# Row-tile pipeline for the self-attention layer norms in a perceiver layer, with the centring moved into the weights

## The chip, the cores and the metric

One core of a Trainium2 chip runs the whole kernel as one launch. The metric is the device time of that launch in microseconds (us). The kernel before took 1715.89 us, the median of 3 runs that lay between 1709.82 and 1721.77. Lower is better.

## The reference

The kernel computes one perceiver layer on 512 latent rows of width 512 and a context of 8192 rows: cross attention with 16 heads of 32, then self attention, then a mixture of 8 experts. The change touches the second step and the weights it uses, so that part is what must be seen:

```python
def layernorm(x, w, b):                      # over the 32 columns of one head
    mu = jnp.mean(x, axis=-1, keepdims=True)
    var = jnp.mean((x - mu) ** 2, axis=-1, keepdims=True)
    return (x - mu) * jax.lax.rsqrt(var + LN_EPS) * w + b
Q = split_heads(jnp.einsum('bsd,od->bso', x, W_Q))
K = split_heads(jnp.einsum('bsd,od->bso', x, W_K))
V = split_heads(jnp.einsum('bsd,od->bso', x, W_V))
Q = layernorm(Q, q_ln_w, q_ln_b)
K = layernorm(K, k_ln_w, k_ln_b)
scores = jnp.einsum('bhqd,bhkd->bhqk', Q, K) / jnp.sqrt(jnp.float32(hd))
attn = jax.nn.softmax(scores, axis=-1)
context = jnp.einsum('bhqk,bhkd->bhqd', attn, V)
v_weights = sparse_W_V.mean(axis=2)          # one vector per head
z = jnp.einsum('bnd,hd->bhn', context_flat, v_weights)
z_sparse = top_k_activation(z, TOP_K)        # the 128 largest of each row
o_weights = sparse_W_O.mean(axis=1)
y_flat = jnp.einsum('bhn,hd->bnd', z_sparse, o_weights)
```

The mean of a head's 32 outputs is linear in the weights: subtracting from every column of the (transposed) weights the mean over its head's 32 columns gives centred outputs.

## The kernel before, in words

The program is a sequence of stages, each a block in which every engine has its own list of instructions, written out in order. A stage begins when every engine has ended the one before. Semaphores alone order the engines among themselves; there is no planner.

- **First pass** (`project_context`): keys and values of the context are projected and stored to DRAM, and the row maxima of the scores are found.
- **Second pass** (`attend_context`, about 572 to 1176 us): for each of 4 groups `g` of 4 heads, 64 tiles `T` of 128 context rows. For each tile TensorE makes the scores (L665), ScalarE takes the exponentials into one of 6 slots of `att_pr` (L748), TensorE multiplies them with the values (L679), and VectorE adds the tile to a running sum of exponentials (`att_tot`, L798, 128 by 2048 elements, both inputs in SBUF). A group has 7 runs of 9 or 10 tiles; the first tile of a run costs no addition, so a 9-tile run has 8 additions. After a run, four tiles later, TensorE sums `att_tot` over its partitions (L695), for which it waits until the additions of that run are done. ScalarE may write a slot only when the addition of the tile six before is done. At a group's end VectorE copies the output out of PSUM (L824) before TensorE may write that bank again. A few tiles into the next group VectorE inverts the sums (L805) and GpSimd multiplies them in (L593, L595). GpSimd also writes the two rows with the next group's maxima into `g_stacks` (L589), which TensorE needs before the next group's first scores.
- **End of the second pass**: after the last additions TensorE sums once more, then computes the output projection and the transposes of the normalised rows (`g_hT`).
- SyncE's queue carries all loads. From 1127 us it loads the sparse weights into `o_yT`, `o_aoT` and `a_woT`, whose buffers have become free (L931, L936).
- **Self projections** (`self_projections`, 1176 to 1241 us): TensorE projects all 4 row tiles of queries (512 rows by 512 outputs), then of keys, then of values (L1001). VectorE centres and normalises each kind as one 128 by 2048 piece (sum L1046, centre L1050, sum of squares L1054, multiply L1058), ScalarE squares it (L1102), TensorE transposes it (L1013), ScalarE applies scale and bias (L1114), VectorE splits it into a rounded part `hi` and a rest `lo` (L1068, L1070). The parts are then copied into `g_stacks` and `a_skst`, 32 partitions for each of 3 places: one place by SyncE's DMAs (L508), one by VectorE (L512), one by ScalarE (L510). VectorE begins the stage with three sums over the sparse weights (L1074, L1076).
- **Self attention** (`self_attend`, from 1241 us): a lead of 20 `whole` steps (L1190), each followed by a row maximum on VectorE (L1278), with two PSUM banks in turn; after each fourth one the head's maxima are turned into rows by TensorE (L1200). Then the exponentials begin (L1258).

## Time and profile before

| | us |
|---|---|
| median of 3 runs | 1715.89 |
| the profiled execution | 1716.72 |
| its span, first to last instruction | 1715.0 |
| busy: TensorE / VectorE / ScalarE / GpSimd | 1551.6 / 1195.3 / 969.8 / 374.4 |

| stage | begins, us | ends, us |
|---|---|---|
| second pass | 572 | 1176 |
| self projections | 1176.6 | 1241.4 |
| lead of self attention, up to the first exponential | 1241.6 | 1260.97 |
| rest of self attention | 1261 | 1364 |

The span of 1715.0 us lies inside a run of 1716.72 us, 1.7 us more, and this run is 0.83 us above the median. TensorE looks busiest by far over the whole span, but that is a mean over stages with different limits: in the second pass VectorE works nearly as long as TensorE, and in the lead of self attention TensorE works at half its clock.

### The profile page before, as it was taken

Reading aid. Unit: us, or ns where it says so; the run is one execution under the profiler, and the core shown is the slowest. Engines: PE = TensorE matmul, PEld = TensorE weight load, DVE = VectorE, ACT = ScalarE, POOL = GpSimd, SP = SyncE. Lnnn points to the kernel's source line nnn. Section 1 sums busy time; section 2 is a strip of 40 time slices with the busy share of each in tenths; the row PEclk is TensorE's granted clock in tenths of the full one; section 3 lists DMA queues with packets and bytes.
Section 4 is the critical chain, followed back from the end, with each engine's and each line's share of the span. In section 5 each row is a group of like instructions: output and inputs, shape, how many; then the busy total and the mean of one; then the engine's idle time right before and its main releaser. Section 6 shows DMA issues by size and latency. Waiting matters only on the chain. (4 is left out here: it accounts for less than half of the span.)

```text
span 1715.0 us, 21707 instructions
## 1 busy us (share of the span) xinstructions
PE 1551.6 (90%) x7992; PEld 820.3 (48%) x7992; DVE 1195.3 (70%) x1834; ACT 969.8 (57%) x1167; POOL 374.4 (22%) x141
## 2 busy tenths in 40 slices
PE   6799999999999799999999999998697407699998
PEld 4466666666665333333333333333353104577775
DVE  5677677677677799999999999995775484120002
ACT  3366666666667688888888888871544401111110
POOL 4463663653650104030021001002000000100001
PEclk9899999999999899999999999998878657799999
DMA  4454354354454544565544444433200360379993
GB/s 171 160 184 168 131 194 161 135 197 151 144 193 120 147 121 114 147 168 145 140 113 124 120 115 117 116 74 49 49 1 1 137 261 2 117 261 326 327 323 112
DMA packets 117337, 250.26 MB, mean 146 GB/s; under 512 B 9705, under 2 KB 26089, under 8 KB 112753
## 3 DMA queue, kind: packets, MB, share of 16 engines
q1 hardware_dynamic: 115520, 244.68, 45.7%
q0 software_dynamic: 1280, 4.20, 0.8%
q8 instruction: 64, 1.05, 0.3%
q14 instruction: 41, 0.33, 0.1%
q10 hardware_dynamic: 432, 0.01, 0.0%
HBM read 182.26 MB, written 61.34 MB: 142 GB/s over the span
## 5 line engine op out<-in xcount | busy, mean ns | idle before, releaser
L748 ACT ACTIVATE att_pr<-att_sc 128x1024 f32<-128x1024 f32 x512 | 496.5, 1022 | 75.0 <-PE att_sc L665 75.0
L798 DVE TENSOR_TENSOR att_tot<-att_tot,att_pr 128x2048 f32<-128x2048 f32 x200 | 467.2, 2336 | 21.9 <-ACT att_pr L748 1.7
L491 DVE CUSTOM_DVE_ANT_0 ctx_size<-ctx_tot,ctx_size 128x512 f32<-128x512 f32 x512 | 333.0, 688 | 134.7 <-PE ctx_tot L411 131.0
L462 ACT ACTIVATE ctx_size<-ctx_dif 128x1024 f32<-128x1024 f32 x256 | 262.4, 1025 | 123.6 <-PE ctx_dif L411 123.6
L665 PE MATMUL att_sc<-g_stacks,att_kst 98*128 98x512 f32 x1024 | 308.9, 424 | 1.5 <-DVE g_stacks L589 1.5
L665 PEld LDWEIGHTS att_sc<-g_stacks,att_kst 98*128 98x128 f32 x1024 | 173.7, 189 | 236.8 <-ACT att_pr L748 211.5
L679 PE MATMUL att_o<-att_pr,att_val 128*32 128x512 f32 x2048 | 273.6, 606 | 2.0 <-issue 1.9
L1749 ACT ACTIVATE ex_hidT<-ex_hp,m_b 128x128 f32<-128x128 f32 x120 | 34.4, 368 | 195.9 <-PE ex_hp L1704 195.9
L411 PE MATMUL ctx_dif<-ctx_k_dif,f_q_hi 32*128 32x512 f32 x512 | 128.5, 498 | 8.7 <-DVE ctx_best L491 4.7
L411 PE MATMUL ctx_tot<-ctx_k_sum,f_q_hi 32*128 32x512 f32 x512 | 128.1, 498 | 0.0
L86 PE MATMUL f_proj<-f_wv_hi,g_stacks 128*128 128x512 f32 x320 | 120.7, 420 | 0.0
L86 PE MATMUL f_proj<-g_stacks,f_wk_hi 128*128 128x512 f32 x352 | 119.5, 421 | 0.8 <-DVE f_k_lo L206 0.8
L1704 PEld LDWEIGHTS ex_hp<-ex_xT,m_w 128*128 128x128 f32 x960 | 109.4, 192 | 8.0 <-issue 8.0
L1704 PE MATMUL ex_hp<-ex_xT,m_w 128*128 128x128 f32 x960 | 109.8, 275 | 0.8 <-issue 0.8
L1717 PE MATMUL ex_yp<-m_w,ex_hidT 128*128 128x512 f32 x240 | 105.5, 592 | 0.0
L411 PEld LDWEIGHTS ctx_dif<-ctx_k_dif,f_q_hi 32*128 32x128 f32 x512 | 47.6, 182 | 105.3 <-issue 52.4
L100 POOL TENSOR_TENSOR g_stacks<-f_raw,g_stacks 128x2048 fp32r<-128x2048 f32 x21 | 96.8, 4608 | 1.7
L679 PEld LDWEIGHTS att_o<-att_pr,att_val 128*32 128x32 f32 x2048 | 40.4, 108 | 96.8 <-issue 95.5
L593 POOL TENSOR_TENSOR o_aoT<-att_whole,att_rs 128x512 f32<-128x512 f32 x3 | 9.4, 3138 | 330.3 <-DVE att_rs L805 330.3
L1757 DVE COPY ex_xT<-ex_tx 128x512 f32<-128x512 f32 x15 | 10.4, 692 | 95.0 <-PE ex_tx L1658 88.8
L86 PEld LDWEIGHTS f_proj<-g_stacks,f_wk_hi 128*128 128x128 f32 x352 | 60.3, 189 | 29.7 <-issue 20.1
L1763 DVE COPY o_yT<-ex_yp 128x512 f32<-128x512 f32 x15 | 10.4, 692 | 91.4 <-PE ex_yp L1717 91.4
(269 smaller groups left out, 1978.3 us busy)
## 6 DMA issues: line engine op xcount, KB each, us to landing
m_w<-in_W SPq DMA_DIRECT2D x30, 2048.0 KB, 13.8
att_kst<-keys_scratch SPq DMA_DIRECT2D x192, 256.0 KB, 3.9
f_raw<-in_ctx SPq DMA_DIRECT2D x32, 1024.0 KB, 5.9
keys_scratch<-f_k_hi SPq DMA_DIRECT2D x32, 512.0 KB, 2.8
keys_scratch<-f_k_lo SPq DMA_DIRECT2D x32, 512.0 KB, 3.2
values_scratch<-ctx_v SPq DMA_DIRECT2D x32, 512.0 KB, 3.3
att_val<-values_scratch SPq DMA_DIRECT2D x64, 256.0 KB, 2.7
rows_scratch<-mix_blank SPq DMA_DIRECT2D x1, 3840.0 KB, 26.5
```

The costliest lines, as they stand in the source:

```text
L86: mm = pe.matmul(out, left, right, start=(n == 0), stop=(n == 3 * len(a) - 1))
L100: pool.tensor_tensor(c.lo[b], raw[:, :, :], f32(c.hi[b]), ALU.subtract).then_inc(c.s_lo, 1)
L411: mm = pe.matmul(out[:, r * CH:(r + 1) * CH], c.q_hi[rows, g, t * P:(t + 1) * P], keys[m % 2][rows, g, :], start=True, stop=True)
L462: act.activation(size[:, i % ABS, :], dif[:, :], ACT.Abs).then_inc(s_size, 1)
L491: dve.tensor_tensor_reduce(out=size[:, i % ABS, r * CH:(r + 1) * CH], in0=tot[i % 2][:, r * CH:(r + 1) * CH], in1=size[:, i % ABS, r * CH: ...
L665: mm = pe.matmul(sc[pair % PAIRS][:, r * N:(r + 1) * N], kst[m % CHUNKS][:, j, at:at + P], c.stacks[0:STK + 2, HG * (T // PER_G) + j, :], ...
L679: mm = pe.matmul(o[at, :], val[m % CHUNKS][:, T % KT, at], pr[:, T % SLOTS, j, :], start=first, stop=False, skip_group_check=True)
L748: act.activation(pr[:, T % SLOTS, 2 * s:2 * s + 2, :], sc[(2 * T + s) % PAIRS][:, :].rearrange("p (j q) -> p j q", j=2), ACT.Exp, scale=SC ...
L798: dve.tensor_tensor(tot[b % 2][:, :, :], so_far, pr[:, T % SLOTS, :, :], ALU.add).then_inc(s_add, 1)
L1704: mm = pe.matmul(hp[tau % 2][:, f, :], w1[b][:, k, f * P:(f + 1) * P], xT[tau % 2][:, k, :], start=(k == 0), stop=(k == DC - 1))
L1717: mm = pe.matmul(yp[tau % 2][:, :], hidT[tau % 2][:, f, :], w2[b][:, f, :], start=(f == 0), stop=(f == FC - 1))
L1749: act.activation(hidT[tau % 2][:, f, :], hp[tau % 2][:, f, :], ACT.Relu, bias=b1[:, f, :]).then_inc(s_hid, 1)
```

## The change

What it does, part by part:

1. **Centring in the weights.** While the second pass runs, GpSimd subtracts from `swqT` and `swkT` the mean over each head's 32 columns (`centre`, called after `weigh` of groups 1 and 2). A mean is a tree of halving additions (`add_up`): 5 additions, one scaling and one subtraction for each of 4 row blocks, so 28 instructions for one matrix.
2. **Row tile by row tile.** In `self_projections` the 8 tiles (4 of queries, 4 of keys) each have a PSUM bank and go one by one through projection, square, sum, root, multiply, transpose, affine and split. Sum and subtraction of the mean are gone, as are the centred copies.
3. **Stacking by DMA.** All copies into `g_stacks` and `a_skst` go over SyncE's queue, except one quarter, which VectorE makes (the second half of the keys, place 0).
4. **Two value tiles in the lead.** Only value tiles 0 and 1 are projected in `self_projections`; tiles 2 and 3 are projected in the lead of `self_attend`, after its `whole` steps 4 and 8, and ScalarE copies them out.
5. **Sparse weights on GpSimd.** The three sums over the sparse weights move from VectorE in `self_projections` to GpSimd in `self_attend`, as halving trees. SyncE loads these weights only after both matrices have been centred.

```diff
+        def centre(pool, n):
+            w = (c.swqT, c.swkT)[n][:, :, :].rearrange("p k (h d) -> p k h d", d=HD)
+            pool.wait_ge((c.sq_in, c.sk_in)[n], 16)
+            pool.wait_ge(s_out, n + 2)
+            done = 7 * DC * n
+            for k in range(DC):
+                ...
+                done = add_up(pool, mean, w[:, k, :, :], room, s_mean, done)
+                pool.wait_ge(s_mean, done)
+                pool.tensor_scalar(mean, mean, 1.0 / HD, None, ALU.mult).then_inc(s_mean, 1)
+                pool.wait_ge(s_mean, done + 1)
+                pool.tensor_tensor(w[:, k, :, :], w[:, k, :, :], mean.unsqueeze(2).broadcast_to([P, H, HD]),
+                                   ALU.subtract).then_inc(s_mean, 1)
...
                 weigh(pool, g)
+                if g:
+                    centre(pool, g - 1)
...
             sp.wait_ge(s_bo, NT)
+            sp.wait_ge(s_mean, 2 * 7 * DC)
             load_mixing(sp, c, s_mm)
...
+def add_up(pool, out, src, room, s_add, done):
+    half = src.shape[-1] // 2
+    pool.tensor_tensor(room[:, :, 0:half], src[:, :, 0:half], src[:, :, half:], ALU.add).then_inc(s_add, 1)
+    while half > 1:
+        half, done = half // 2, done + 1
+        pool.wait_ge(s_add, done)
+        dst = room[:, :, 0:half] if half > 1 else out.unsqueeze(2)
+        pool.tensor_tensor(dst, room[:, :, 0:half], room[:, :, half:2 * half], ALU.add).then_inc(s_add, 1)
+    return done + 1
...
             # self_projections, TensorE
-            for t in range(NT):
-                mm = project(queries, c.swqT, t)
-            mm.then_inc(s_raw, 1)
...
+            for n in range(TILES):
+                if n == NT:
+                    pe.wait_ge(c.sk_in, 16)
+                project(raw[n], c.swkT if n >= NT else c.swqT, n % NT).then_inc(s_raw, 1)
+                if n >= 2:
+                    turn(n - 2)
+            turn(TILES - 2)
+            values(0)
+            turn(TILES - 1)
+            values(1)
...
             # SyncE
+            for n, cols, done in ((0, slice(0, N), NT), (1, slice(0, HALF), NT + NT // 2), (1, slice(HALF, N), TILES)):
+                _, places, place = STACKS[n]
+                sp.wait_ge(s_hi, done)
+                for at in places:
+                    if not (n and at == 0 and done == TILES):
+                        copies(n, hi[n], at, cols)
+                sp.wait_ge(s_lo, done)
+                copies(n, lo[n], place, cols)
...
             # VectorE
+            for n in range(TILES):
+                dve.wait_ge(s_sq, n + 1)
+                dve.tensor_reduce(spread[:, n, :], heads(sq[:, n % 2, :]), AX.X, ALU.add).then_inc(s_spread, 1)
+                ...
+                if 3 <= n < TILES - 1:
+                    split(n - 3)
+                ...
+                dve.tensor_tensor(heads(nrm[:, n % 2, :]), heads(raw[n][:, :]), wide(rstd[:, n, :]), ALU.mult).then_inc(s_nrm, 1)
+            for n in range(TILES - 4, TILES):
+                split(n)
...
             # self_attend, TensorE
+                if i in (HG, 2 * HG):
+                    values(NT // 2 + i // HG - 1, (o, den)[i // HG - 1])
```

Three places in the order of instructions. The first is GpSimd in the second pass, from `weigh` of group 1 (L593, L595) to `weigh` of group 2; `o_yT` is scratch and `a_swqT` the query weights. Before:

```order
L593 TENSOR_TENSOR o_aoT<-att_whole,att_rs 128x512
L595 TENSOR_SCALAR o_aoT<-o_aoT,g_bv 128x512
L589 CAST g_stacks<-o_yT 2x512 x4
L593 TENSOR_TENSOR o_aoT<-att_whole,att_rs 128x512
L595 TENSOR_SCALAR o_aoT<-o_aoT,g_bv 128x512
```

And now, the first of the four row blocks:

```order
L593 TENSOR_TENSOR o_aoT<-att_whole,att_rs 128x512
L595 TENSOR_SCALAR o_aoT<-o_aoT,g_bv 128x512
L952 TENSOR_TENSOR o_yT<-a_swqT 128x256
L957 TENSOR_TENSOR o_yT<-o_yT 128x16x8
L957 TENSOR_TENSOR o_yT<-o_yT 128x16x4
L957 TENSOR_TENSOR o_yT<-o_yT 128x16x2
L957 TENSOR_TENSOR o_yT<-o_yT 128x16
L608 TENSOR_SCALAR o_yT<-o_yT 128x16
L610 TENSOR_TENSOR a_swqT<-a_swqT,o_yT 128x512
```

These 7 stand four times between `weigh` of group 1 and the four CASTs that write group 3's maxima rows, and four times more on `a_swkT` after `weigh` of group 2.

The second place is SyncE's queue in `self_projections` (`sp_hi` and `sp_lo` are the two parts). Before:

```order
L508 DMA g_stacks<-sp_hi 32x4x512 x4
L508 DMA a_skst<-sp_hi 32x4x512 x4
```

And now:

```order
L1028 DMA g_stacks<-sp_hi 32x4x512 x8
L1028 DMA g_stacks<-sp_lo 32x4x512 x4
L1028 DMA a_skst<-sp_hi 32x4x256 x8
L1028 DMA a_skst<-sp_lo 32x4x256 x4
L1028 DMA a_skst<-sp_hi 32x4x256 x4
L1028 DMA a_skst<-sp_lo 32x4x256 x4
```

8 DMAs have become 32: 12 of 256 KB and 20 of 128 KB.

The third place is TensorE at the end of the projections and in the lead of self attention (`sa_o` and `sa_den` are two PSUM banks, here lent to the value tiles). Before:

```order
L1001 MATMUL sp_keys<-a_swvT,g_hT 128x512 x8
L957 UNCONDITIONAL_BRANCH
L1183 UNCONDITIONAL_BRANCH
L1190 MATMUL sa_full<-a_skst,g_stacks 128x512 x8
L1200 MATMUL sa_rows<-g_ident,sa_shift 98x128 x4
```

And now:

```order
L1044 MATMUL sp_raw<-a_swvT,g_hT 128x512 x4
L995 UNCONDITIONAL_BRANCH
L1166 UNCONDITIONAL_BRANCH
L1179 MATMUL sa_full<-a_skst,g_stacks 128x512 x5
L1170 MATMUL sa_o<-a_swvT,g_hT 128x512 x4
L1179 MATMUL sa_full<-a_skst,g_stacks 128x512 x3
L1189 MATMUL sa_rows<-g_ident,sa_shift 98x128 x4
L1179 MATMUL sa_full<-a_skst,g_stacks 128x512
L1170 MATMUL sa_den<-a_swvT,g_hT 128x512 x4
```

The four matrix products of a value tile now stand behind the first 5 `whole` steps and again behind the ninth; before, the lead held none.

## Rows read from the trace of the kernel before

**Rows 1.** The page, part 5: a group's busy time, mean ns; idle before it, what ended it.
```profile
L798 DVE TENSOR_TENSOR att_tot<-att_tot,att_pr 128x2048 f32<-128x2048 f32 x200 | 467.2, 2336 | 21.9 <-ACT att_pr L748 1.7
```

**Rows 2.** Three stretches: busy us of each engine, then granted clock, DMA share, GB/s.
```profile
1114.00:1154.00 40.00, 39.88 (x229) 14.80 (x228) 36.87 (x17) 33.33 (x34) 0.00 (x0) 1.00 0.33 79
1217.00:1222.00 5.00, 4.02 (x11) 1.52 (x10) 4.61 (x5) 3.24 (x3) 0.00 (x0) 1.00 0.92 203
1241.50:1260.00 18.50, 16.27 (x38) 9.34 (x39) 15.36 (x37) 2.69 (x5) 0.00 (x0) 0.50 0.00 0
```

**Rows 3.** GpSimd in order of time, second pass: start us, us, then the instruction.
```profile
638.88 12.55 POOL L604 TENSOR_TENSOR g_x<-g_x,o_yT 128x512 f32<-128x512 f32 x4 [61.58 <-DMA o_yT<-in_bo]
...
887.49 3.14 POOL L593 TENSOR_TENSOR o_aoT<-att_whole,att_rs 128x512 f32<-128x512 f32 x1 [123.81 <-DVE att_rs L805]
890.72 3.49 POOL L595 TENSOR_SCALAR o_aoT<-o_aoT,g_bv 128x512 f32<-128x512 f32 x1
896.21 10.38 POOL L589 CAST g_stacks<-o_yT 2x512 fp32r<-2x512 f32 x4 [2.00 <-DVE o_yT L817]
```

**Rows 4.** VectorE's additions in order of time, beside GpSimd's work and without it.
```profile
646.92 3.37 DVE L798 TENSOR_TENSOR att_tot<-att_pr 128x2048 f32<-128x2048 f32 x1
...
887.27 8.21 DVE L798 TENSOR_TENSOR att_tot<-att_tot,att_pr 128x2048 f32<-128x2048 f32 x3
...
896.00 2.28 DVE L798 TENSOR_TENSOR att_tot<-att_pr 128x2048 f32<-128x2048 f32 x1
898.38 17.55 DVE L798 TENSOR_TENSOR att_tot<-att_tot,att_pr 128x2048 f32<-128x2048 f32 x7
...
918.23 16.67 DVE L798 TENSOR_TENSOR att_tot<-att_tot,att_pr 128x2048 f32<-128x2048 f32 x7
...
984.75 7.08 DVE L798 TENSOR_TENSOR att_tot<-att_tot,att_pr 128x2048 f32<-128x2048 f32 x3
```

**Rows 5.** VectorE and GpSimd in order of time, 22 to 28 us, both reading SBUF.
```profile
23.15 4.89 DVE L203 TENSOR_TENSOR g_hT<-prep_h,f_q_hi 128x512 f32<-128x512 f32 x1
...
22.92 4.58 POOL L100 TENSOR_TENSOR f_third<-f_raw,f_third 128x2048 fp32r<-128x2048 f32 x1
```

**Rows 6.** VectorE in order of time, 990 to 1154 us; idle before, its releaser, in brackets.
```profile
992.51 2.29 DVE L798 TENSOR_TENSOR att_tot<-att_pr 128x2048 f32<-128x2048 f32 x1 [0.68 <-ACT att_pr L748]
...
1011.49 0.69 DVE L824 COPY att_whole<-att_o 128x512 f32<-128x512 f32 x1
...
1115.04 2.29 DVE L798 TENSOR_TENSOR att_tot<-att_pr 128x2048 f32<-128x2048 f32 x1 [0.76 <-ACT att_pr L748]
...
1135.03 2.29 DVE L798 TENSOR_TENSOR att_tot<-att_pr 128x2048 f32<-128x2048 f32 x1 [0.92 <-ACT att_pr L748]
```

**Rows 7.** TensorE's weight loads in order of time, the last sum of the pass.
```profile
1154.55 0.16 PEld L695 LDWEIGHTS att_den<-att_tot,g_ones 128*32 128x32 f32 x8 [0.76 <-DVE att_tot L798]
```

**Rows 8.** Self projections in order of time, four engines and SyncE's queue.
```profile
1176.62 16.76 PE L1001 MATMUL sp_queries<-a_swqT,g_hT 128*128 128x512 f32 x32 [1.11 <-PEq L542]
...
1193.22 13.90 PE L1001 MATMUL sp_keys<-a_swkT,g_hT 128*128 128x512 f32 x32
...
1200.24 2.29 DVE L1054 TENSOR_REDUCE sp_spread<-sp_nrm 128x64 f32<-128x2048 f32 x1 [1.98 <-ACT sp_nrm L1102]
...
1206.95 1.91 PE L1013 MATMUL sp_queries<-g_ident,sp_nrm 128*128 128x128 f32 x16
...
1215.55 3.40 SPq L508 DMA_DIRECT2D g_stacks<-sp_hi  x4
...
1223.73 7.03 PE L1001 MATMUL sp_keys<-a_swvT,g_hT 128*128 128x512 f32 x16
...
1239.73 1.08 ACT L1123 ACTIVATE a_sval<-sp_keys 128x512 f32<-128x512 f32 x2
```

**Rows 9.** The lead of self attention in order of time, its first matmuls and first exponentials.
```profile
1241.58 1.22 PE L1190 MATMUL sa_full<-a_skst,g_stacks 96*128 96x512 f32 x2 [10.82 <-DVE sa_shift L1265]
...
1260.97 1.08 ACT L1258 ACTIVATE sa_pr<-sa_sc 128x512 f32<-128x512 f32 x2
```

More of the change, by code:

```diff
@@ L995, in _, with copies @@
-            sp.wait_ge(s_copy_dma, 16 * 2 * HG)
+            def copies(n, part, place, cols):
+                for j in range(HG):
+                    sp.dma_start(f32(rows(n, place, j, cols)), f32(part[HD * j:HD * j + HD, :, cols])).then_inc(s_copy_dma, 16)
+            for n, cols, done in ((0, slice(0, N), NT), (1, slice(0, HALF), NT + NT // 2), (1, slice(HALF, N), TILES)):
[6 more added lines that the diff above has]
+                copies(n, lo[n], place, cols)
@@ L1020, in _ @@
[L1020 to L1031 removed]
+                    mm = pe.transpose(raw[n][:, g * P:(g + 1) * P], nrm[:, n % 2, g * P:(g + 1) * P], c.ident[:, :])
@@ L1184, in _, with values @@
         def _(pe):
+            def values(t, bank):
+                for k in range(DC):
+                    mm = pe.matmul(bank[:, :], c.hT[:, k, t * P:(t + 1) * P], c.swvT[:, k, :],
+                                   start=(k == 0), stop=(k == DC - 1))
+                mm.then_inc(s_v, 1)
             def whole(i):
```

251 lines of the change are left out of this document (110 added, 141 removed).

## Prediction, made before the changed kernel was run

> **What bounds the kernel now.** The views were read from coarse to fine. The page's busy times show TensorE far ahead, which says little, because every stage has its own limit. Its groups show VectorE's additions in the second pass as one of the largest, 200 of 2336 ns, with 1.7 us of waiting put down to ScalarE in all of them [rows 1]. So the next view is the busy time by stretch, and then the instructions in order of time in the three stages that the change touches.
>
> In the second pass TensorE and ScalarE set the pace, but with little to spare. From 1114 to 1154 us TensorE is busy 39.88 of 40 us and VectorE 36.87 [rows 2]. Its additions follow one another every 2.38 us (seven in 16.67 us [rows 4]) and need 19.0 us for the 8 of a nine-tile run, while the run takes 20.0 us (1135.03 against 1115.04 [rows 6]). The reader should see there how seldom VectorE waits for an exponential: after 894 us only three times, for 0.68, 0.76 and 0.92 us, apart from some 0.6 us at the start of the last group, which stays there whatever happens. And the pass ends on VectorE: TensorE's last sum waits 0.76 us for the last addition [rows 7]. So whatever delays VectorE in the pass by more than 2.4 us in all delays its end.
>
> The self projections last from 1176.6 to 1241.4 us. TensorE is done at 1230.8 (1223.73 and 7.03); the stage's last work is ScalarE's copying of stacks and values, to 1240.8 [rows 8]. The lead of self attention runs at a granted clock of 0.50, the 1.2 GHz level, after TensorE had been idle for 10.8 us; within it TensorE is busy 16.27 of 18.5 us and VectorE 15.36 [rows 2, 9].
>
> **Centring on GpSimd in the second pass.** While GpSimd works, VectorE's additions get longer: one beside the last of L604's additions of 128x512 took 3.37 us in place of 2.28 [rows 4], three beside L593 and L595 took 8.21 in place of 7.08, and seven beside the four CASTs 17.55 in place of 16.67. GpSimd suffers too: its 128x512 operations take 3.1 to 3.5 us and the CASTs 2.6 each, one for each addition of VectorE [rows 3]. The two take turns. So VectorE loses about 1.0 us for a two-input operation of 512 elements, 0.1 for a scaling (1.13 less 1.0) and 0.22 for a CAST. That the loss goes by elements is seen at 23 us, where VectorE's 128x512 operation took 4.89 us beside GpSimd's 2048-element one of 4.58 [rows 5]; it takes 0.7 alone (L824, as large [rows 6]), so it lost 4.2 us, or 2.05 ns an element.
>
> A row block of `centre` has additions over 256, 128, 64, 32 and 16 elements and a subtraction over 512, 1008 in all, which is 1008 / 512 x 1.0 = 2.0 us, and one scaling, 0.1: 2.1 us. Four of these are 8.2 us for a matrix, and 16.4 for both. Bounds: if only the two largest of each block count, 768 elements, 1.5 x 8 = 12 us; if each of the five smaller instructions costs at least a CAST's 0.22, then (1.0 + 0.5 + 5 x 0.22) x 8 = 21 us. A cost of 1.09 for each of the 56 instructions would be 61 us, but the CASTs cost a fifth of that, so I keep it for a rival. The Trainium skill (SBUF — State Buffer, section "Who interferes with whom") has VectorE with two SBUF inputs and a reading GpSimd exclude one another; by that rule the loss is GpSimd's whole time, and the trace agrees. The Trainium skill (GPSIMD Engine Reference) gives 4497 ns for 2048 elements; as an estimate, 8064 elements would by it cost 17.7 us, 1.3 more than the sum has.
>
> What absorbs it: the 0.68 us before 1011 us, when TensorE waits for VectorE's copy at the group's end and the delay becomes the pass's own, and the 0.76 and 0.92 after the second matrix. 16.4 - 2.4 = **+14 us** (range 9.6 to 18.6). The runs' sums come late in the same measure and TensorE and ScalarE wait; I do not count that again. Queued behind `centre(0)` are the CASTs for group 3. 28 instructions at 2.6 to 3.5 us last 73 to 98 us from 894.3, the CASTs 10.4 more, so the rows are there by 978 to 1003 us, and TensorE wants them about 1009.7 (copy at 1011.49, two score pairs earlier), and later by then. SyncE's new wait ends near 1045 + 80 = 1125 us, about when the loads begin now (1127); they are not needed until self attention.
>
> **Self projections.** TensorE's list: 8 tiles, 16.76 + 13.90 us as before, since the first ones again run at the low clock, and transposes of 1.91 / 4 = 0.48 a tile. VectorE's work for a tile is about 2.9 us (a quarter of 2.29 for each of sum and multiply, and 1.1 for the split), ScalarE's 1.6, against TensorE's 3.47 + 0.48: TensorE is the bound. The removed centring, a sum and a subtraction of 2.29 us for each kind, leaves VectorE's chain; the three sums for the sparse weights, as large, were hidden behind the query projections before and free nothing. Projection of tile 6 ends at 1176.6 + 16.76 + 3 x 3.47 + 4 x 0.48 = 1205.7, and two us later, after square, sum and the cast of tile 3, the first stacking DMA starts: 1207.8. TensorE has all done at about 1218.4.
>
> Then the copies end last. 12 DMAs of 256 KB and 20 of 128 KB are 3.15 + 2.62 = 5.77 MB. The four of 256 KB before moved at 203 GB/s with the DMA engines 0.92 busy [rows 2], so 221 GB/s when full: 26.1 us. With 1.5 us to start and 1 to land the last, 1236.4, and 0.8 us to the next stage as now (1240.8 to 1241.58): it begins at 1237.2, **-4 us**. Bounds: issuing alone, 32 at 3.40 / 4 = 0.85 with a slow first, or 0.65 behind it, gives 20.8 us and a landing 3.5 later, 1232, -9; if a 128 KB DMA of 1 KB rows takes as long as one of 256 KB with 2 KB rows, 11.9 us more, +7. I take the middle, because it rests on the same kind of copy. The Trainium skill (SBUF — State Buffer, "The DMA setup-cost knee") fits 2 us and 436 GB/s to a transfer; as an estimate 5.77 MB would then take 13.2 us, issuing would be the bound and this term -9. The row shows half that rate for copies of 32 partitions.
>
> **The lead.** A value tile is 13.90 / 4 = 3.5 us at the high clock and 7.0 at 1.2 GHz. TensorE has idled here for 18 us as it had for 10.8 before, so the first tile runs at the low level (7.0) and, after it, I expect the high one for the second (3.5), as in the query projections. From these 10.5 us go 1.3, the maxima that VectorE takes meanwhile, and about 1, since the later heads' turns run faster: **+8 us** (5 if both tiles run fast and overlap, 13 if both are slow). The moved tiles were no longer on the path of the projections once the copies end it, so nothing comes back for them. GpSimd's sums for the sparse weights, 3 x 2032 elements, lie mostly under those tiles; VectorE reads PSUM for its maxima, and its three small operations a head may wait for GpSimd, 0 to 3 us. I price it at 0 because the value tiles hide the largest ones; if they didn't, +3.
>
> **Sum.** 14 - 4 + 8 = +18 us on the profiled 1716.7, 1734.7; the median lies 0.8 lower, so **1734 us**.
>
> **Rivals.** (a) *The contention is hidden*: VectorE's delays stay in the slots of `att_pr` and never reach TensorE. Against it speak VectorE's few waits and the wait at the end [rows 6, 7]. The first term falls away: 1720 us. Chance 0.17.
> (b) *The projections end with TensorE*, the other side: if the copies move at over twice 221 GB/s, the stage ends at 1219.2, 22 us sooner, not 4. The point from which it decides is 5.77 MB within 11 us. With (a) as well it is 1716 + 0 - 22 + 5 = 1699 us. The rate of the copies before speaks against it [rows 2]. Chance 0.06.
> (c) *GpSimd falls behind*: it gets in at every second addition only. 28 x 4.8 + 10.4 = 145 us from 894, so group 3's rows come at 1039, 29 us late, and the key weights after their use would begin. 1734 + 29 = 1763 us or more. The four CASTs, which also wait on one another, got in at every addition, which speaks against it. Chance 0.07.
> (d) *The change does not shorten the projections*, since 1 KB rows are slow: 1745 us. Chance 0.15.
> The forecast as it stands: 0.55.
>
> **Numbers.** About 1% (17 us, 1733) is what a measurement of this kernel can tell from no change. The forecast lies on that line; of its 0.55 I give 0.28 to slower and 0.27 to the same. With (c) and (d) slower has 0.50, with (a) the same has 0.44, faster 0.06. The range takes in (a) and (d) with their bounds and the forecast's own 1722 to 1748: 1714 to 1750 us.
>
> **What would show it.** In the changed profile: additions (L798, now some twenty lines on) near 2.75 us on average beside `centre`; ScalarE or the sums waiting for `att_tot` after 920 us, and the pass's end near 1168; 28 GpSimd instructions in 75 to 95 us; in the projections a DMA share over 0.9 from 1222 to 1250 and TensorE idle behind its last value tile; a lead of 27 us in place of 19. It is wrong if the pass ends within 3 us of 1154, or if the copies land sooner than 25 us after the first.

## The result, and the profile after

The changed kernel takes 1728.84 us (median of 11 runs, 1720.60 to 1733.12) against 1715.89 us for the kernel before (median of 11 runs in the same comparison, 1709.82 to 1722.73). The ratio is 1.0066, with a 95% interval of 1.0049 to 1.0083: 0.7% slower, 13 us: clear of the scatter, but under the 1% that was called no change. 1734 us had been forecast, in a range of 1714 to 1750. Two runs, one of the kernel before (7752.17 us) and one of *copies shared* (2193.83 us), were in a far slower state and are left out of the ratios.

The profiled execution took 1730.99 us, its span 1728.9 (before: 1716.72 and 1715.0). The table cuts both spans, and those of the experiments, at the same instructions, in us: *start* is GpSimd's first memset of the second pass, *pass* goes from there to the first matmul of the self projections, *projections* to the first score matmul of self attention, *lead* to its first exponential; the *rest* of self attention, the sparse step (*mix*), the router and the experts follow.

| kernel | start | pass | projections | lead | rest | mix | router | experts | span |
|---|---|---|---|---|---|---|---|---|---|
| before | 571.9 | 604.7 | 65.0 | 19.4 | 93.8 | 85.3 | 44.0 | 230.9 | 1715.0 |
| after | 572.9 | 613.0 | 60.1 | 26.3 | 93.3 | 85.1 | 45.4 | 232.8 | 1728.9 |
| no centring | 574.4 | 604.7 | 61.2 | 25.0 | 93.1 | 83.5 | 45.4 | 233.0 | 1720.3 |
| centring in small parts | 574.3 | 606.3 | 60.9 | 25.1 | 93.1 | 83.7 | 45.4 | 233.0 | 1721.8 |
| before with the centring | 566.6 | 614.0 | 64.6 | 19.4 | 93.5 | 85.1 | 45.5 | 233.2 | 1721.8 |
| queries' centring only | 570.1 | 610.1 | 61.0 | 25.1 | 93.2 | 83.7 | 45.4 | 233.0 | 1721.6 |
| keys' centring only | 568.7 | 607.8 | 60.3 | 25.9 | 93.5 | 85.2 | 44.0 | 230.9 | 1716.2 |
| value tiles back | 570.4 | 613.4 | 60.3 | 24.1 | 93.1 | 83.6 | 45.5 | 232.9 | 1723.2 |
| value tiles back, sums on VectorE | 569.8 | 612.8 | 61.7 | 19.4 | 96.3 | 83.6 | 45.5 | 233.1 | 1722.1 |
| sums on VectorE | 570.3 | 613.4 | 62.3 | 25.3 | 91.3 | 83.5 | 45.5 | 232.8 | 1724.4 |
| copies shared | 571.7 | 613.5 | 50.2 | 19.1 | 93.5 | 85.0 | 45.5 | 232.8 | 1711.3 |
| copies shared, small parts | 572.3 | 605.9 | 50.6 | 19.1 | 93.9 | 85.1 | 45.4 | 232.8 | 1705.1 |

What a reader should see first: the three stages that the change touches moved by +8.3, -4.9 and +6.9 us, +10.3 together. The start, the mix, the router and the experts differ between executions whose code is the same there (566.6 to 574.4, 83.5 to 85.3, 44.0 or 45.5, 230.9 or 233): a difference of several us between two spans says nothing by itself, and a stage is to be compared with a stage. The touched stages scatter too. *After*, *no centring*, *small parts*, *queries' only* and *keys' only* have the same instructions in the projections and in the lead, and took 60.1 to 61.2 and 25.0 to 26.3 us there; so the change's -4.9 and +6.9 stand for -3.8 to -4.9 and +5.6 to +6.9.

**The second pass.** VectorE's additions, as the page after groups them (as [rows 1]), and four windows of the pass (columns as in [rows 2]):

```profile
L819 DVE TENSOR_TENSOR att_tot<-att_tot,att_pr 128x2048 f32<-128x2048 f32 x200 | 474.9, 2375 | 24.5 <-ACT att_pr L769 4.3
```

```profile
1004.00:1010.00 6.00, 6.00 (x36) 2.39 (x36) 5.74 (x3) 5.55 (x6) 0.00 (x0) 1.00 0.23 72
1012.50:1016.50 4.00, 0.16 (x1) 0.00 (x0) 3.90 (x4) 1.67 (x2) 0.00 (x0) 0.87 0.26 66
1016.60:1022.40 5.80, 5.77 (x21) 1.63 (x21) 3.72 (x2) 1.96 (x2) 0.00 (x0) 0.51 0.00 0
1023.00:1029.00 6.00, 6.00 (x39) 2.21 (x41) 4.69 (x4) 5.48 (x6) 0.00 (x0) 1.00 0.69 175
```

The first line has 200 additions 39 ns longer each, 7.7 us in all, and 2.6 us more of waiting for ScalarE. The second view has the place of that waiting, the end of the second group: TensorE, busy all the time until there, does nothing for 4 us and then works at a granted clock of 0.51, the 1.2 GHz level.

GpSimd in order of time, beginning with the last instruction of the first row block of the query weights; then one whole block, the subtraction of the next, the casts of group 3's rows, and the last subtraction of the key weights (columns as in [rows 3]):

```profile
908.90 3.10 POOL L610 TENSOR_TENSOR a_swqT<-a_swqT,o_yT 128x512 f32<-128x512 f32 x1
912.09 2.67 POOL L952 TENSOR_TENSOR o_yT<-a_swqT 128x256 f32<-128x256 f32 x1
914.84 9.40 POOL L957 TENSOR_TENSOR o_yT<-o_yT 128x128 f32<-128x128 f32 x4
924.33 2.34 POOL L608 TENSOR_SCALAR o_yT<-o_yT 128x16 f32<-128x16 f32 x1
926.75 3.11 POOL L610 TENSOR_TENSOR a_swqT<-a_swqT,o_yT 128x512 f32<-128x512 f32 x1
...
965.43 10.40 POOL L589 CAST g_stacks<-o_yT 2x512 fp32r<-2x512 f32 x4
...
1111.06 3.11 POOL L610 TENSOR_TENSOR a_swkT<-a_swkT,o_yT 128x512 f32<-128x512 f32 x1
```

And VectorE beside it (as [rows 4, 6]): seven additions beside a row block, seven without GpSimd, and what follows the second group's end; last its copy at the pass's end.

```profile
919.48 17.75 DVE L819 TENSOR_TENSOR att_tot<-att_tot,att_pr 128x2048 f32<-128x2048 f32 x7
...
980.28 16.67 DVE L819 TENSOR_TENSOR att_tot<-att_tot,att_pr 128x2048 f32<-128x2048 f32 x7
...
1015.84 0.68 DVE L845 COPY att_whole<-att_o 128x512 f32<-128x512 f32 x1
...
1020.81 2.29 DVE L819 TENSOR_TENSOR att_tot<-att_tot,att_pr 128x2048 f32<-128x2048 f32 x1 [2.08 <-ACT att_pr L769]
1024.20 7.09 DVE L819 TENSOR_TENSOR att_tot<-att_tot,att_pr 128x2048 f32<-128x2048 f32 x3 [1.10 <-ACT att_pr L769]
...
1163.75 0.68 DVE L845 COPY att_whole<-att_o 128x512 f32<-128x512 f32 x1
```

A row block costs GpSimd 17.86 us (from the end of one L610 to the end of the next, 926.75 + 3.11 against 908.90 + 3.10), one instruction for each of VectorE's additions, and costs VectorE 1.1 to 1.2 us (17.75 against 16.67, and 17.86 against the 16.67 that seven additions take alone). Four blocks from 895.1 us to the casts at 965.4 last 70 us, less than the 73 to 98 forecast. TensorE at the group's end, and at the end of the pass, where [rows 7] had a wait of 0.76 us:

```profile
1011.46 1.20 PE L686 MATMUL att_sc<-g_stacks,att_kst 98*128 98x512 f32 x4
1016.63 1.93 PE L700 MATMUL att_o<-att_pr,att_val 128*32 128x512 f32 x8 [3.97 <-issue]
1018.49 2.08 PE L686 MATMUL att_sc<-g_stacks,att_kst 98*128 98x512 f32 x4
```

```profile
1163.89 0.16 PEld L716 LDWEIGHTS att_den<-att_tot,g_ones 128*32 128x32 f32 x8 [3.06 <-DVE att_tot L819]
```

**Self projections** (columns as in [rows 8, 9]): the first query matmuls, SyncE's copies in the order in which they are issued, the last value tile in this stage, and the first score matmuls of self attention with TensorE's wait before them.

```profile
1185.96 12.34 PE L1044 MATMUL sp_raw<-a_swqT,g_hT 128*128 128x512 f32 x24 [1.11 <-PEq L542]
...
1215.70 7.95 SPq L1028 DMA_DIRECT2D g_stacks<-sp_hi  x8
1223.70 3.93 SPq L1028 DMA_DIRECT2D g_stacks<-sp_lo  x4
1227.68 5.83 SPq L1028 DMA_DIRECT2D a_skst<-sp_hi  x8
...
1238.73 2.53 SPq L1028 DMA_DIRECT2D a_skst<-sp_lo  x4
...
1222.24 3.60 PE L1044 MATMUL sp_raw<-a_swvT,g_hT 128*128 128x512 f32 x8
...
1246.03 1.22 PE L1179 MATMUL sa_full<-a_skst,g_stacks 96*128 96x512 f32 x2 [20.20 <-DVE sa_shift L1294]
```

```profile
1217.00:1222.00 5.00, 5.00 (x20) 2.68 (x19) 3.55 (x9) 2.45 (x5) 0.00 (x0) 1.00 0.98 215
1226.00:1245.00 19.00, 0.00 (x0) 0.00 (x0) 1.47 (x3) 0.47 (x1) 0.00 (x0) 0.62 1.07 205
1246.00:1272.00 26.00, 23.02 (x55) 12.11 (x56) 18.45 (x36) 4.53 (x7) 19.65 (x32) 0.70 0.00 0
```

TensorE is done at 1225.84 (1222.24 and 3.60) and waits 20.20 us. All this time the DMA engines are full (share 0.98 to 1.07, 205 to 215 GB/s) and the other engines all but empty: the copies end the stage. SyncE issues its last DMA at 1241.26, and 4.8 us later the next stage begins. From 1232 to 1242 us, when at the rate seen the 3.15 MB of the 256 KB copies were through and only 128 KB ones were left, they moved 217 GB/s.

**The lead**: the two value tiles and the first exponentials. The first tile takes 5.91 us and the second 3.60.

```profile
1249.78 5.91 PE L1170 MATMUL sa_o<-a_swvT,g_hT 128*128 128x512 f32 x8
...
1257.72 3.60 PE L1170 MATMUL sa_den<-a_swvT,g_hT 128*128 128x512 f32 x8
...
1272.32 1.09 ACT L1257 ACTIVATE sa_pr<-sa_sc 128x512 f32<-128x512 f32 x2
```

### The profile page after: what moved, and what is told of

Same layout as the page of the kernel before. It is cut to its first block and busy times, and to the rows that moved or that the text cites. A ratio compares the mean times of both kernels' runs of the same rounds, so it can differ in the third digit from the quotient of the medians.

```text
span 1728.9 us, 21837 instructions
## 1 busy us (share of the span) xinstructions
PE 1554.3 (90%) x7992; PEld 821.4 (48%) x7992; DVE 1188.8 (69%) x1840; ACT 956.3 (55%) x1171; POOL 527.9 (31%) x223
## 5 line engine op out<-in xcount | busy, mean ns | idle before, releaser
L819 DVE TENSOR_TENSOR att_tot<-att_tot,att_pr 128x2048 f32<-128x2048 f32 x200 | 474.9, 2375 | 24.5 <-ACT att_pr L769 4.3
L593 POOL TENSOR_TENSOR o_aoT<-att_whole,att_rs 128x512 f32<-128x512 f32 x3 | 9.4, 3141 | 267.7 <-DVE att_rs L826 267.7
L98 POOL CAST g_stacks<-f_raw 128x2048 fp32r<-128x2048 f32 x21 | 39.9, 1900 | 124.0 <-DMA f_raw<-in_ctx 86.5
L1677 POOL DMA_INDIRECT g_stacks<-back_scratch,m_slot x8 | 7.6, 951 | 221.2 <-DMA back_scratch<-o_yT 219.0
```

Source lines behind the costliest of these rows:

```text
L98: pool.tensor_copy(c.hi[b], raw[:, :, :]).then_inc(c.s_hi, 1)
L819: dve.tensor_tensor(tot[b % 2][:, :, :], so_far, pr[:, T % SLOTS, :, :], ALU.add).then_inc(s_add, 1)
```

## The experiments

All times are compared with the kernel before, run on the same chip in the same comparison (its median there lay between 1716.83 and 1718.70 us); stages are those of the table, each from one profiled execution.

### Is the pass's loss GpSimd's centring?

*No centring.* The changed kernel without the means taken from the weights, so queries and keys are normalised with their mean left in:

```diff
                 weigh(pool, g)
-                if g:
-                    centre(pool, g - 1)
...
-            sp.wait_ge(s_mean, 2 * 7 * DC)
```

> The changed kernel without the 56 centring instructions in the second pass (the weights stay uncentred, so queries and keys are normalised without their mean taken away). Theory: in the changed kernel the second pass lasts 613.0 us against 604.7 before, 8.3 more, because VectorE's additions lose 4.3 us to each matrix. Without them the pass is back at 604.7 us and the kernel 8 to 9 us below the changed one, near 1720 us. Rival: the pass is longer for another reason (group 3's rows later, SyncE's new wait); then it stays near 613.

Measured: 1720.91 us (12 runs), ratio 1.0011 (0.9997 to 1.0026). The pass is back at 604.7 us. The seven additions after 920 us:

```profile
920.76 16.67 DVE L816 TENSOR_TENSOR att_tot<-att_tot,att_pr 128x2048 f32<-128x2048 f32 x7
```

*Before with the centring.* The other way round: `centre`, its calls and SyncE's wait put into the kernel before, all else as it was.

```diff
                 weigh(pool, g)
+                if g:
+                    centre(pool, g - 1)
...
+            sp.wait_ge(s_mean, 2 * 7 * DC)
```

> The kernel before with the centring of the changed kernel added on GpSimd in the second pass, and nothing else (its projections centre once more, which then changes nothing). Theory: the second pass lasts 8.3 us more than before, 613 us, all other stages as before, 1724 us in all. Rival: the centring costs only beside the rest of the change; then it is at 1716.

Measured: 1726.14 us (11 runs), ratio 1.0048 (1.0032 to 1.0063). The pass is 614.0 us, +9.3. So the whole of the pass's loss, 8.3 to 9.3 us, is the centring, taken away or put in.

### Which part of it costs?

*Small parts.* The 256-element addition is cut in two and the 512-element subtraction in four, each of at most 128 elements: 11 instructions a block, 88 in all. Both matrices are centred in group 2, after GpSimd has written the rows of group 3.

```diff
-                done = add_up(pool, mean, w[:, k, :, :], room, s_mean, done)
+                for half in range(2):
+                    hs = slice(H // 2 * half, H // 2 * half + H // 2)
+                    pool.tensor_tensor(room[:, hs, 0:16], w[:, k, hs, 0:16], w[:, k, hs, 16:32], ALU.add)...
...
-                pool.tensor_tensor(w[:, k, :, :], w[:, k, :, :], ...
+                for q in range(4):
+                    hs = slice(4 * q, 4 * q + 4)
+                    pool.tensor_tensor(w[:, k, hs, :], w[:, k, hs, :], ...
...
+                if g == 2:
+                    centre(pool, 0)
                 pool.wait_ge(s_rs, g + 1)
                 weigh(pool, g)
-                if g:
-                    centre(pool, g - 1)
+                if g == 2:
+                    centre(pool, 1)
```

> The changed kernel with the centring cut into instructions of at most 128 elements: the addition over 256 becomes two, the subtraction over 512 four, 11 instructions a row block in place of 7, 88 in all, over the same 8064 elements; group 3's rows are written before the first matrix is centred. Theory (cost by size, and nothing below some size: in the changed kernel the additions beside GpSimd's instructions of up to 128 elements kept their pitch of 2.38 us): VectorE loses nearly nothing, the pass is back at 605 to 607 us, the kernel 6 to 9 below the changed one. Rival (cost by element, 1.17 us a block whatever the cut): the pass stays at 613. Second rival (cost by instruction, 0.17 each for 7): 1.84 us a block, the pass near 618 us.

Measured: 1721.43 us (12 runs), ratio 1.0013 (0.9998 to 1.0027); the pass takes 606.3 us. GpSimd's four tree additions and four quarters of the subtraction, then VectorE's additions beside them:

```profile
914.67 9.33 POOL L615 TENSOR_TENSOR o_yT<-o_yT 128x128 f32<-128x128 f32 x4
...
926.52 9.67 POOL L622 TENSOR_TENSOR a_swqT<-a_swqT,o_yT 128x128 f32<-128x128 f32 x4
```

```profile
921.63 16.71 DVE L833 TENSOR_TENSOR att_tot<-att_tot,att_pr 128x2048 f32<-128x2048 f32 x7
```

The same elements are added and subtracted by GpSimd, in 88 instructions instead of 56, and these seven additions of VectorE take 16.71 us instead of 17.75. They are the mildest: the next three sevens take 16.82, 16.90 and 16.86. The whole of it is in the sums. The 48 additions that end with the copy at the second group's end take 110.4 us in the kernel before, 112.1 with small parts and 114.7 in the changed kernel; the 57 behind that copy take 131.4, 133.1 and 136.0:

```profile
L833 DVE TENSOR_TENSOR att_tot<-att_tot,att_pr 128x2048 f32<-128x2048 f32 x200 | 468.9, 2344 | 22.7 <-ACT att_pr L783 2.5
```

So a matrix costs VectorE 1.7 to 1.8 us in small parts where it cost 4.3 and 4.7, and the loss goes neither by elements, as I had it, nor by instructions. It is nearly nothing up to 128 elements, and each larger instruction costs what it sticks out by. With the pitches of GpSimd in the changed kernel: an addition of VectorE comes every 2.38 us; the four small additions of a block take 9.40 us, 2.35 each, and the scaling 2.34: nothing lost in all. From the L952 to the next instruction is 2.75 us (914.84 less 912.09), 0.37 over 2.38; from the L610 it is 3.18 (the next L952 is at 929.94), 0.80 over. That is 1.17 us a block and 4.7 for a matrix, 4.3 for the queries', whose first L952 took 1.72 us only. Instructions of exactly 128 elements do cost something: the six that replace the L952 and the L610 come every 2.44 us or so, 0.06 to 0.09 over each, which makes the 0.4 us a block of the small parts. (The first matrix is also begun 14 us later in this kernel, at 909.7 us, but it too is done by the group's end.) Of their 3.4 us, 2.4 fall into waits that VectorE had in the kernel before (0.68, 0.76 and 0.92), so the pass is 1.6 longer and not 3.4. The expectation, 605 to 607 us, held, and both of its rivals are refuted.

At the second group's end VectorE's copy is at 1015.84 against 1011.49 in [rows 6]: 4.35 us later, 1.0 of which its pass began later, and 0.68 had been absorbed on the way, so its delay was 4.0.

### Is there more than VectorE's delay?

*One matrix only.* In two kernels one centring is left out, that of the keys' weights and that of the queries'; the mean stays in the kind left out.

```diff
-                if g:
-                    centre(pool, g - 1)
+                if g == 1:
+                    centre(pool, 0)
```

> The changed kernel with only the query weights centred (behind group 1's weighing); the keys' centring is left out. Theory: VectorE loses 4.3 us, 0.7 of it is absorbed before the group's end, and there 2.4 us more are lost, since TensorE has waited for VectorE's copy of the group's output and VectorE then waits 2.5 us longer for the next exponentials; by the end 1.7 us are absorbed: pass 604.7 + 4.3 - 0.7 + 2.4 - 1.7 = 609.0 us. Rival (nothing is lost at the group's end): 606.6 us.

```diff
-                if g:
-                    centre(pool, g - 1)
+                if g == 2:
+                    centre(pool, 1)
```

> The changed kernel with only the key weights centred (behind group 2's weighing); the queries' centring is left out. Theory: VectorE loses 4.3 us, 1.7 are absorbed, no group's end follows but the last: pass 604.7 + 2.6 = 607.3 us. Rival (the loss of a matrix is always its share of 8.3 us): 608.9.

Measured: queries only 1725.45 us (8 runs), ratio 1.0058 (1.0036 to 1.0079), pass 610.1, +5.4; keys only 1720.42 us (8 runs), ratio 1.0018 (0.9997 to 1.0039), pass 607.8, +3.1. They add up to 8.5, against 8.3 for both. The theory had passes of 609.0 and 607.3 and its rivals 606.6 and 608.9, so both measured passes lie nearer to the theory, the queries' 1.1 us above it. The two matrices have the same instructions but unlike prices, and the difference is at the second group's end. VectorE there, with the queries' centring ahead of it and without:

```profile
1012.59 0.68 DVE L845 COPY att_whole<-att_o 128x512 f32<-128x512 f32 x1
...
1017.56 2.29 DVE L819 TENSOR_TENSOR att_tot<-att_tot,att_pr 128x2048 f32<-128x2048 f32 x1 [2.08 <-ACT att_pr L769]
1020.74 9.52 DVE L819 TENSOR_TENSOR att_tot<-att_tot,att_pr 128x2048 f32<-128x2048 f32 x4 [0.89 <-ACT att_pr L769]
```

```profile
1008.20 2.29 DVE L819 TENSOR_TENSOR att_tot<-att_pr 128x2048 f32<-128x2048 f32 x1 [0.32 <-ACT att_pr L769]
1010.81 11.88 DVE L819 TENSOR_TENSOR att_tot<-att_tot,att_pr 128x2048 f32<-128x2048 f32 x5 [0.31 <-ACT att_pr L769]
```

TensorE needs VectorE's copy of a group's output before it writes the next group's. While VectorE is on time that is no wait (0.41 us in the kernel without centring). With the queries' centring ahead of it TensorE idles 3.96 us, and its next matmuls run at the low clock, as the four windows above show for the changed kernel: 1.93 us for eight instead of 1.07, until 1022.4. So the exponentials come late, ScalarE's and then VectorE's, which had been the late one, waits 3.0 us where it waited 0.63. That is 2.3 us that no centring instruction took. The slow matmuls account for it: in the changed kernel TensorE starts again 4.35 us later than in the kernel before (1016.63 against 1012.28), but ScalarE's next exponentials are 5.71 us later (1019.75 against 1014.04) and so is VectorE's next addition (1020.81 against 1015.10), 1.36 us more, behind the first ten slow matmuls. With the small parts TensorE idles 1.37 us here and its next eight matmuls take 1.06: no low clock.

### What do the value tiles and GpSimd's sums cost in the lead?

*Value tiles back*: all four are computed in the projections, by TensorE and ScalarE; GpSimd's sums for the sparse weights stay beside the lead.

```diff
-            values(1)
+            for t in range(1, NT):
+                values(t)
...
-                if i in (HG, 2 * HG):
-                    values(NT // 2 + i // HG - 1, (o, den)[i // HG - 1])
```

> The changed kernel with all four value tiles in the self projections. Theory: TensorE idles there for 20 us until the stacking DMAs land, so the two tiles cost nothing, the stage stays at 60.1 us, and the lead, 26.3 us from its first matmul to the first exponential, goes back to 19 to 20: the kernel 6 to 7 us below the changed one. Rival: the tiles warm TensorE's clock in the lead and hide GpSimd's sums, so that without them the lead shortens by less than 4 us.

Measured: 1727.56 us (6 runs), ratio 1.0063 (1.0042 to 1.0083); the lead is 24.1 us. That falls outside what was expected, and sent me to the instructions. VectorE and GpSimd in the lead of this kernel:

```profile
1247.73 0.61 DVE L1309 TENSOR_SCALAR sa_shift_hi<-g_neg 128x4 fp32r<-128x4 f32 x1
...
1252.44 1.22 DVE L1312 SCALAR_TENSOR_TENSOR sa_shift<-g_neg,sa_shift_hi 128x4 f32<-128x4 f32 x1
...
1256.47 1.98 DVE L1309 TENSOR_SCALAR sa_shift_hi<-g_neg 128x4 fp32r<-128x4 f32 x1
```

```profile
1246.26 3.31 POOL L957 TENSOR_TENSOR sa_room<-sa_room 128x512 f32<-128x512 f32 x5
...
1249.94 2.36 POOL L952 TENSOR_TENSOR sa_room<-a_woT 128x1024 f32<-128x1024 f32 x1
1252.38 3.32 POOL L957 TENSOR_TENSOR sa_room<-sa_room 128x512 f32<-128x512 f32 x5
```

*Value tiles back, sums on VectorE*: the same, and the three sums again on VectorE, as in the kernel before, between the tiles of the projections.

```diff
+                if n in (2, 3):
...
+                    dve.tensor_reduce(om[...], wo[n - 2], AX.X, ALU.add).then_inc(s_om, 1)
+                if n == 4:
+                    dve.tensor_reduce(vm[:, :], wv, AX.X, ALU.add).then_inc(s_vm, 1)
```

> The changed kernel with all four value tiles in the self projections, as in the run before, and the three sums over the sparse weights on VectorE, one each behind its third, fourth and fifth row tile there; GpSimd has nothing in the lead. In the run before the lead lasted 24.1 us where 19.4 were expected, and VectorE's small operations took up to 1.22 us in place of 0.15 beside GpSimd's sums. Theory: GpSimd's sums hold VectorE's small operations, 4.7 us in all; the lead is back at 19.4 us, the projections stay within 1 us of 60.3. Rival: the lead is longer for the clock, after a longer idle time of TensorE; then it stays near 24.

*Sums on VectorE*: the same move of the sums, with the two value tiles left in the lead; the cut is against the kernel just above.

```diff
+                if i in (HG, 2 * HG):
+                    values(NT // 2 + i // HG - 1, (o, den)[i // HG - 1])
```

> The changed kernel with the three sums on VectorE in the projections, and the two value tiles left in the lead. The price of the tiles alone: theory 19.4 + 5 to 7 = 24.4 to 26.4 us for the lead, since most of GpSimd's hold lay under the value tiles (26.3 us with both). Rival, the two add up: 26.3 - 4.7 = 21.6 us.

Measured: 1727.55 us (8 runs), ratio 1.0059 (1.0039 to 1.0079), lead 19.4; and 1727.16 us (7 runs), ratio 1.0057 (1.0035 to 1.0079), lead 25.3. Of the first the theory held in the lead and missed in the projections, which took 61.7 us where 59.3 to 61.3 were expected; of the second the theory held (24.4 to 26.4) and the rival (21.6) fell. Without GpSimd at work the same operations of VectorE take 0.16 and 0.17 us; the line is the view of `sa_shift` in the kernel without value tiles in its lead (lowest, middle and highest ns of 16):

```profile
L1307 DVE SCALAR_TENSOR_TENSOR sa_shift<-g_neg,sa_shift_hi x16: 155/155/160, 1248.3 to 1327.8; 128x4 f32<-128x4 f32 x16
```

The lead has fifteen such operations, three for each of five heads. They take 7.6 us in all with GpSimd's sums beside them and 2.5 without, and the difference of 5.2 us covers the 4.7 of the lead; the reductions of `sa_full`, which read PSUM, take 0.68 us in both.

The four corners of the lead are 19.4 us (neither), 24.1 (sums alone), 25.3 (tiles alone) and, with both, 25.0 to 26.3 in the five kernels that have the same lead. Each alone costs much, +4.7 and +5.9, but they cover one another: what the sums add to the lead with the tiles there can't be told from the scatter. Over the lead and the rest together they do show: 118.1 to 119.6 us with both, 116.6 with the tiles alone. The scatter of the lead comes from TensorE's clock, which rises at different moments within the first value tile: it takes 4.61 us in the kernel without centring and 5.91 in the changed one.

The medians show less than the lead: taking the sums off GpSimd gained 4.7 us in it and nothing in the whole (ratios 1.0063 and 1.0059). VectorE's three sums cost the projections 1.4 us, little more than their scatter, and the rest of self attention takes 96.3 us for 93.1. Most of these 3.2 us lie behind the last group's end, from which the rest takes 19.4 us here and 17.0 with the values back alone. TensorE waits there for VectorE in each of these kernels. In the one with the short lead:

```profile
1340.48 1.94 PE L1237 MATMUL sa_o<-sa_pr,a_sval 128*32 128x512 f32 x8 [2.62 <-DVE o_aoT L1295]
...
1348.03 1.93 PE L1241 MATMUL sa_den<-sa_pr,g_ones 128*32 128x512 f32 x8
```

Eight matmuls take 1.06 us at the high clock. After the same wait of 2.62 us they ran at the low one for 9.4 us here (to 1349.9), and for 5.6 in the kernel before (1337.29 to 1342.93) and with the copies shared, whose rest is 93.5 us. Why the clock stays low longer here is not settled.

### Can the projections be ended sooner?

*Copies shared.* To the kernel with all values and sums back in the projections, against which the cut is shown: the queries' three places and the keys' third go by 32 DMAs of 128 KB, each half as soon as its tiles are there (4.2 MB for 5.77 MB); VectorE copies the keys' place 0 in four whole rows and ScalarE their place 1 in eight halves.

```diff
+            halves = (slice(0, HALF), slice(HALF, N))
+            for half in range(2):
+                sp.wait_ge(s_hi, 2 * half + 2)
+                copies(0, hi[0], 0, halves[half])
+                copies(0, hi[0], 1, halves[half])
+                sp.wait_ge(s_lo, 2 * half + 2)
+                copies(0, lo[0], 2, halves[half])
+            for half in range(2):
+                sp.wait_ge(s_hi, NT + 2 * half + 2)
+                copies(1, hi[1], 2, halves[half])
...
-                dve.tensor_copy(rows(1, 0, j, slice(HALF, N)), ...
+                dve.tensor_copy(rows(1, 0, j, slice(0, N)), ...
...
+                for j in range(HG):
+                    act.activation(rows(1, 1, j, cols), f32(lo[1][HD * j:HD * j + HD, :, cols]), ACT.Copy)...
```

> The kernel of e7_sums_dve with the stacking shared out: the queries' copies by DMA in halves, from the second row tile on; of the keys, place 0 by VectorE, the low parts by ScalarE, place 2 by DMA. Theory (the copies' 5.8 MB at about 220 GB/s end the stage): DMAs carry 4.2 MB and start 7.7 us sooner, so the stage ends when ScalarE does, at 49 to 52 us in place of 60; the lead 19.4. Rival (the stage is bound by issuing, 0.64 us a DMA, of which there are as many): 57 us or more.

Measured: 1713.37 us (10 runs), ratio 0.9974 (0.9956 to 0.9993). The projections take 50.2 us, 10 less than after the change, 15 less than before and 11.5 less than the kernel that it was made from; 49 to 52 had been expected. Two things changed at once, and are not told apart: the DMAs carry 1.6 MB less, and the first starts 23.7 us into the stage and not 31.3. 22 of the stage's last 26 us have TensorE and VectorE busy nearly throughout and the DMA engines at 0.82:

```profile
1209.00:1231.00 22.00, 21.01 (x65) 10.22 (x64) 20.41 (x37) 13.55 (x20) 0.62 (x3) 1.00 0.82 188
```

*Copies shared, small parts.* This and the centring in small parts together; no other edit.

> The kernel of e5_copies with the centring in instructions of at most 128 elements, as in e2_small. If the terms add up: pass 606.3, projections 50, lead 19.4, all else as before: 1716 + 1.6 - 15 + 0 = 1703 us, below both kernels. Rival: a faster projection stage meets the loads of the sparse weights, which are sent only after the centring; then the projections take 55 us or more.

Measured: 1706.01 us (6 runs, 1698.52 to 1709.10), ratio 0.9928 (0.9899 to 0.9956), 12 us faster by the ratio than the kernel before: it beats both. 1703 had been expected, from a pass of 606.3, projections of 50 and a lead of 19.4; the stages are 605.9, 50.6 and 19.1, and the rival, projections of 55 us or more behind late loads, fell. SyncE's queue, the shared copies on VectorE and ScalarE, and TensorE at the end of the stage:

```profile
1202.30 5.41 SPq L1045 DMA_DIRECT2D g_stacks<-sp_hi  x8
...
1218.16 5.14 SPq L1045 DMA_DIRECT2D a_skst<-sp_hi  x8
...
1218.29 4.95 DVE L1127 CAST a_skst<-sp_hi 32x2048 fp32r<-32x2048 f32 x4
...
1222.15 4.29 ACT L1168 ACTIVATE a_skst<-sp_lo 32x1024 fp32r<-32x1024 f32 x4
...
1228.81 0.74 PE L1231 MATMUL sa_full<-a_skst,g_stacks 96*128 96x512 f32 x2 [2.14 <-DVE sa_shift L1310]
```

The last DMA is issued at 1223.3, the last copy of ScalarE ends at 1226.4 and TensorE's last value tile at 1226.7. It waits 2.14 us where it waited 20.20, and its first two score matmuls take 0.74 us where the changed kernel's took 1.22. Three engines and the queue now end within 4 us of one another.

## Why the prediction was right, and where it was not

**The sum.** Forecast were +14, -4 and +8, +18 together. The stages have +8.3, -4.9 and +6.9, +10.3. The median moved by 13.0: the spans differ by 13.9, of which +1.0 lies before the pass, +1.4 in the router and +1.9 in the experts, where no instruction changed and where kernels of either kind show either value. So the forecast of 1734 us was 5 us too high. The three terms were 7.7 us too high together, 5.7 of it by the first; that only 5 show is luck, since stages that the forecast left alone took 3.6 us more, and a part of the true 13 us may be such scatter.

**The pass, +14 against +8.3: mis-sized.** The mechanism held: VectorE's additions lengthen beside GpSimd, the pass ends on VectorE, and TensorE's wait at the end grows (3.06 us for 0.76). Rival (a), contention hidden in the slots of `att_pr`, is refuted by the two kernels that add and remove the centring alone. The step that failed is the price: "about 1.0 us for a two-input operation of 512 elements", carried to the smaller ones by "the loss goes by elements". 1008 elements were to cost 2.1 us a block and cost 1.17. The rows behind it were additions of 128x512 (3.37 us for 2.28 [rows 4]) and one of 2048 at 23 us [rows 5], scaled down to sizes that neither row has. The 496 elements of a block in sizes up to 256 were priced at 1.0 us and cost 0.37, the subtraction at 1.0 and cost 0.80, the scaling at 0.1 and cost nothing. That elements alone don't set the loss could have been read from the casts: they too have 512 elements a partition and cost 0.22 each [rows 4].

The Trainium skill (SBUF — State Buffer, "Who interferes with whom") has it that VectorE with two inputs in SBUF "contends with a GpSimd instruction that reads SBUF", and calls the shared pair an exclusive lock. The trace agrees that the two take turns, once for each of VectorE's instructions. What the prediction concluded from it, that VectorE loses the whole of GpSimd's time, is not so here for 128 elements and less, where seven additions took 16.71 to 16.90 us for 16.67.

A second step failed the other way: "the delay becomes the pass's own" at the group's end. It becomes more. TensorE's wait there is long enough (3.97 us) that its granted clock falls, and VectorE, 4 us late, then waits 3.2 us instead of 0.6. The ledger: 4.3 and 4.7 us of VectorE's delay for the two matrices, less the 0.68 and 1.68 forecast as absorbed, plus 2.5 at the group's end (2.08 and 1.10 less the 0.63), is 9.1; measured 8.3. 8.3 lies below the term's own range, which began at 9.6: the price was 7.4 us too high for both matrices, and the 2.5 at the group's end, which the prediction put at nothing, made up a part.

**GpSimd keeps up.** 28 instructions in 70 us, forecast 73 to 98. Rival (c), in at every second addition, is refuted by each of the rows: one instruction for each of VectorE's additions, in all sizes up to 512. SyncE's loads were free to start at 1114.2 us (the last subtraction, 1111.06 and 3.11), for the 1125 forecast.

**The projections, -4 against -4.9: right, and for the reason given.** The copies end last, at 205 to 217 GB/s where 221 had been worked out, and TensorE idles behind its last value tile. The first DMA started 29.7 us into the stage (1215.70 less 1185.96; forecast 31.2) and the stage lasted 60.1 us (60.6). Both bounds fell: rival (b), projections that end with TensorE, would need twice the rate, and rival (d), rows of 1 KB that are slow, is refuted by 217 GB/s through the stretch of 128 KB copies. That the copies hold the stage is shown by giving some of them to other engines and starting the others sooner: 10 us.

**The lead, +8 against +6.9: right.** The two tiles alone made it +5.9 (25.3 against 19.4): 9.0 us of work in that kernel (5.42 and 3.60) less 3.1, where the sum had 10.5 less 2.3. In the changed kernel they took 5.91 and 3.60 us for 7.0 and 3.5, and moving them back freed nothing in the projections (60.3 us for 60.1), as the prediction said. GpSimd's sums were priced at 0 under the tiles' cover, and no more than the scatter is seen of them in the lead; without that cover they were to cost 3 and cost 4.7. The wait for GpSimd of VectorE's three small operations had been named, but its size was taken too low, and I repeated it in the expectation of the experiment with the value tiles back, which missed for that.

**What stays open.** Why the gain in the lead is lost again behind it (TensorE's clock behind the last group's end, above), and what makes the price rise so steeply between 128 elements and 256: no size between them was run. Nor is it known how much of the 10 us of the shared copies is their size and how much their earlier start.

## What to carry to other kernels

Where a second engine is put to work beside an elementwise engine that has no slack, read the other one's delay by instruction size before scaling it: here the same work delayed VectorE by 8.9 us with instructions of up to 512 elements, and the pass by 8.3, and in pieces of at most 128 by 3.4 and 1.6. Look then at the next hand-over behind the delayed engine, because a short wait of TensorE can also cost clock: here 2.5 us behind a wait of 3.97. And where the DMA engines are full at the end of a stage while every compute engine idles, a part of the copies belongs on those engines. The new order of the stage with nearly all copies on the DMA engines was worth 5 us here (what of it is the copies', and what the rest of the change, was not run), and with shared copies 15.

## What the hardware did that was not expected

- **GpSimd beside VectorE's two-input additions of 2048 elements** gets in exactly once for each. Beside them an addition or scaling of 16 to 128 elements takes about 2.35 us. It costs VectorE under 0.1 us, one of 256 elements 0.37 us, one of 512 elements 0.80 us.
- **Small operations suffer most.** VectorE's operations of 4 elements a partition took up to 1.98 us beside GpSimd's additions, and 0.15 to 0.17 without them; 4.7 us over a stage of 20 us. Its reductions out of PSUM took 0.68 us in both.
- **Behind a wait of 3.97 us TensorE's granted clock, 1.00 before it, was 0.51 for 5.8 us**; behind a wait of 1.37 us at the same place eight matmuls took 1.06 us. In self attention a wait of 2.62 us was followed by 5.6 us at the low clock in the kernel before and by 9.4 in *value tiles back, sums on VectorE*.
- **Copies within SBUF over 32 partitions** ran at 205 to 217 GB/s with the DMA engines full, no slower with rows of 1 KB (217) than with rows of 2 KB (203 to 215). The Trainium skill (SBUF — State Buffer, "The DMA setup-cost knee") fits 436 GB/s to a transfer; the measurement has half.
